# A graph network on one core: edge terms are placed in the ring and the gathers add node rows to them

## The chip, the cores and the metric

The kernel runs on one core of a Trainium2 chip. Its time is the device time of one execution, in microseconds (us); lower is better. The time before is the median of three runs. Engines are named as in the profile: PE is the matrix engine (PEld its weight loads), DVE the vector engine, ACT the scalar engine, POOL the engine that issues the gathers, SP the engine that only issues transfers.

## What is computed

A layer norm with a ReLU, an encoder, three message passing layers over 212,500 edges of 12,500 nodes, and an output product over all four hidden states, with a residual:

```python
h = jnp.maximum(_layernorm(x), 0.0)
h_list = [h @ enc_w + enc_b]
for l in range(3):
    e = edge_attr @ edge_w[l] + edge_b[l]            # 212500 x 128 from 212500 x 16
    msg = relu(h_list[l][src] + e)
    agg = segment_sum(msg, dst, num_segments=12500)  # edges are sorted by dst
    z = (1.0 + eps[l]) * h_list[l] + agg
    z = relu(z @ mlp_w1[l] + mlp_b1[l]) @ mlp_w2[l] + mlp_b2[l]
    h_list.append(relu(z))
out = x + concatenate(h_list) @ out_w + out_b
```

Everything is float32.

## The kernel before

**Tiling.** The edges are cut into tiles of 128, and four tiles make a group (`TG`), so a layer has `NG` = 416 groups, the last with one tile, and three layers have 1248 groups and 4983 tiles. Node sums live transposed in SBUF (`agg_t`, 128 features by 12,500 nodes). The edges of a group are sorted by destination and fall in a window of 64 nodes (`WIN`) that begins at a base read from a table.

**A group's work.** (1) SP loads the edge attributes, eight groups at a time (`attr`, two halves). (2) POOL gathers the source rows from `h_table` in HBM, one indirect transfer per tile (L372), into a slot of `rows`, a ring of `RING` = 16 slots. (3) PE multiplies the attributes by the edge weights into a PSUM bank (`edge_terms`, L620; three banks `e_ps`). (4) DVE adds the bank to the gathered rows in place (`add_terms`, L879) and makes a one-hot matrix of the destinations (`one_hot`, L865). (5) ACT applies the ReLU in place (L543). (6) PE multiplies the rows by the one-hot matrix, four tiles summed in one bank (`window_sums`, L624; two banks `agg_ps`). (7) DVE adds the 64 columns to `agg_t` (`add_window`, L875).

**Order.** Each engine's order is written by hand; a body of 16 groups is looped on all engines but POOL, whose 416 groups are written out. In a body of before PE does the edge terms of group k+2 and then the sums of group k. DVE does the one-hot matrix of group k, then `add_window` of group k-2, then `add_terms` of group k, so these three wait in that order for one another. POOL waits, before the first tile of a group, for the sums of the group 16 back (semaphore `agg_done`), since they free the slot.

**Node work.** When all edges of 512 nodes are summed, a table says so and the three products of those nodes are put into the same loops (a unit of node work: PE `node_z`, `node_h`, `node_out`; ACT `relu_z`, `relu_h`; DVE `node_take`). Two banks, `zh_ps` and `zt_ps`, serve it. The new node rows go to the other `h_table` by a transfer that ACT issues. The next layer's gathers wait for all of them (semaphore `stored`).

**Start.** After the layer norm the first eight groups of layer 0 are gathered while the encoder's products (`h0_turned`, `o0`) run; the next eight wait for tables that DVE makes (`find_units`, L813); the seventeenth waits for the first group's sums.

## Time and profile before

| | us |
|---|---|
| median of 3 runs | 7389.25 (7386.51 to 7396.62) |
| the profiled execution's own time | 7395.73 |
| its span, first to last instruction | 7393.9 |

| engine | busy us | share |
|---|---|---|
| PE | 4774.5 | 65% |
| POOL | 4751.3 | 64% |
| PEld | 3131.3 | 42% |
| DVE | 1663.8 | 23% |
| ACT | 999.7 | 14% |

The mean granted clock of PE is 0.558 of full speed: most stretches are at the lower of its two levels. Transfers keep the 16 DMA engines busy for about a fifth of the span. No engine is busy for the whole span, so the shares alone do not name the bound; the waits and the timeline do. An engine's idle time stands in square brackets behind the instruction that it waited to begin, with what ended it; "remote" is a release that the profile cannot pin on an instruction, and "issue" is time in which it sees nothing that was waited for. The ends of PE's instructions are modelled, not measured.

### The profile page before, as it was taken

To read this page: it belongs to the slowest core of one execution; us is meant where nothing else is said; L and a number is where in the kernel's file an instruction comes from. 1 tells how busy PE (TensorE), PEld (TensorE's weight loads), DVE (VectorE), ACT (ScalarE), POOL (GpSimd) and SP (SyncE) were. 2 spreads that over 40 slices of the span, in tenths; PEclk is the share of its full clock that TensorE was granted. 3 is DMA by queue.
4 is the path that set the end of the run, shared out by engine and by line. 5 is a ranking of instruction groups with operands and counts; after the bars stand their busy time and mean duration, and the time that the engine had idled before them with its cause. 6 is when DMAs were issued, how large, how long until landed. Compare 5 with 4: busy or idle time off the path is not lost.

```text
span 7393.9 us, 56283 instructions
## 1 busy us (share of the span) xinstructions
PE 4774.5 (65%) x14396; PEld 3131.3 (42%) x14397; DVE 1663.8 (23%) x4168; ACT 999.7 (14%) x1597; POOL 4751.3 (64%) x5075
## 2 busy tenths in 40 slices
PE   5666666666666646666666666673666666666667
PEld 4444444444444424444444444442444444444444
DVE  4222222222222212222222222221222222222222
ACT  4111111111111101111111111110111111111111
POOL 5666666666666466666666666646666666666664
PEclk7555555555555555555555555555555555555555
DMA  3122212222222112222222222211111111111112
GB/s 116 53 54 54 55 53 54 54 55 54 54 54 54 44 49 54 55 55 54 54 55 55 53 54 56 55 43 51 51 51 52 51 52 51 52 51 51 52 52 72
DMA packets 191126, 404.82 MB, mean 55 GB/s; under 512 B 85159, under 2 KB 87927, under 8 KB 190439
## 3 DMA queue, kind: packets, MB, share of 16 engines
q0 software_dynamic: 159456, 326.88, 17.0%
q1 hardware_dynamic: 21759, 56.75, 2.6%
q10 hardware_dynamic: 9840, 20.48, 0.8%
q14 instruction: 55, 0.45, 0.0%
q8 instruction: 16, 0.26, 0.0%
HBM read 378.08 MB, written 25.69 MB: 55 GB/s over the span
## 4 chain that ended last, share of the span: by engine, by line
another core or an unknown queue 44%; PE 27%; issue 18%; DVE 6%; DVEq 3%; ACT 3%; POOL 0%; DMA 0%; ACTq 0%
PE bank L624 14%; PE bank L620 9%; DVE rows L879 3%; ACT rows L543 2%; DVE onehot L865 2%; PE bank L651 1%; PE bank L664 1%; PE bank L643 1%; DVEq L939 1%; DVE agg_t L875 1%; PE bank L645 1%; DVEq L247 1%; DVEq L875 0%; PE bank L661 0%
## 5 line engine op out<-in xcount | busy, mean ns | idle before, releaser
L372 POOL DMA_INDIRECT rows<-h_table,idx x4983 | 4714.0, 946 | 2575.5 <-issue 1417.7
L624 PEld LDWEIGHTS bank<-onehot,rows 128*128 128x128 f32 x9966 | 2178.6, 310 | 3367.3 <-ACT rows L543 1966.2
L624 PE MATMUL bank<-onehot,rows 128*128 128x64 f32 x9966 | 2158.1, 394 | 2162.8 <-ACT rows L543 1599.7
L620 PE MATMUL bank<-edgew,attr 65*128 65x512 f32 x2496 | 2279.0, 1026 | 9.6 <-DMA w2s<-w 9.6
L543 ACT ACTIVATE rows<-rows 128x512 f32<-128x512 f32 x1248 | 783.1, 628 | 5381.1 <-DVE rows L879 4213.0
L875 DVE TENSOR_TENSOR agg_t<-bank,agg_t 128x64 f32 x1248 | 278.1, 223 | 4790.4 <-remote 3542.9
L879 DVE TENSOR_TENSOR rows<-bank,rows 128x512 f32<-128x512 f32 x1248 | 857.6, 687 | 83.2 <-DMA rows<-h_table,idx 35.2
L620 PEld LDWEIGHTS bank<-edgew,attr 65*128 65x128 f32 x2496 | 677.7, 316 | 280.6 <-issue 280.6
L865 DVE TENSOR_TENSOR onehot<-bank,dst_rel 128x256 f32<-128x256 f32 x1248 | 518.3, 415 | 205.4 <-issue 205.4
L651 PE MATMUL bank<-hid,w2s 128*128 128x512 f32 x300 | 195.3, 769 | 192.5 <-ACT hid L506 124.8
L664 PE MATMUL bank<-outw,h_t 128*128 128x128 f32 x588 | 151.7, 423 | 62.0 <-ACT h_t L515 58.5
L506 ACT ACTIVATE hid<-bank,b1s 128x512 f32<-128x512 f32 (+1 forms) x150 | 101.0, 678 | 539.1 <-remote 297.3
L664 PEld LDWEIGHTS bank<-outw,h_t 128*128 128x128 f32 x588 | 142.5, 326 | 64.2 <-ACT h_t L515 60.4
L651 PEld LDWEIGHTS bank<-hid,w2s 128*128 128x128 f32 x300 | 59.8, 233 | 256.5 <-ACT hid L506 155.7
L643 PE MATMUL bank<-agg_t,w1s 128*128 (+1 forms) x150 | 149.1, 1097 | 1.7 <-DVE agg_t L875 1.7
L645 PE MATMUL bank<-agg_t,w1s 128*128 (+1 forms) x150 | 124.5, 928 | 0.0
L661 PE MATMUL bank<-ident,h_t 128*128 128x128 f32 x196 | 45.6, 372 | 107.2 <-ACT h_t L515 100.7
L916 DVE COPY h_n<-bank 128x512 f32<-128x512 f32 (+1 forms) x50 | 34.1, 681 | 356.3 <-remote 242.8
L515 ACT ACTIVATE h_t<-bank,b2s 128x512 f32<-128x512 f32 (+1 forms) x75 | 50.9, 678 | 369.1 <-remote 232.3
L922 DVE TENSOR_TENSOR out_acc<-bank,out_acc 128x512 f32 (+1 forms) x75 | 50.6, 674 | 199.3 <-remote 101.8
L645 PEld LDWEIGHTS bank<-agg_t,w1s 128*128 128x128 f32 x150 | 50.3, 335 | 74.9 <-issue 74.4
L661 PEld LDWEIGHTS bank<-ident,h_t 128*128 128x128 f32 x196 | 33.7, 224 | 112.1 <-ACT h_t L515 104.8
(83 smaller groups left out, 478.6 us busy)
## 6 DMA issues: line engine op xcount, KB each, us to landing
rows<-h_table,idx POOLq DMA_INDIRECT x4983
attr<-ea_t SPq DMA_DIRECT2D x156, 256.0 KB
h_table<-h_n ACTq DMA_DIRECT2D x48, 256.0 KB
h_table<-rows SPq DMA_DIRECT2D x24, 256.0 KB, 2.1
out<-out_acc SPq DMA_DIRECT2D x24, 256.0 KB
out_acc<-x_t ACTq DMA_DIRECT2D x4, 1280.0 KB, 11.5
rows<-dst_g SPq DMA_DIRECT2D x1, 832.0 KB
rows<-dst_t SPq DMA_DIRECT2D x1, 832.0 KB
```

The costliest lines, as they stand in the source:

```text
L372: return g.indirect_dma_start(dst, None, h_table[l % 2], bass.IndirectOffsetOnAxis(ap=index, axis=0))
L506: nc.scalar.activation(hid[:, c, 0:cols], ps[:, 0:cols], ACT.Relu, bias=b1s[:, l * HC + c:l * HC + c + 1])\
L543: nc.scalar.activation(part, part, ACT.Relu).then_inc(relued, 1)
L620: return nc.tensor.matmul(dst[0:EP, 0:tiles * D], cols, edgew[:, l, 0:tiles * D], start=True, stop=True)
L624: last = nc.tensor.matmul(dst[:, 0:WIN], rows[0:EP, slot, j, :], onehot[0:EP, hot_slot, j, :], start=(j == 0), stop=(j == tiles - 1))
L643: nc.tensor.matmul(zh_ps[:, 0:cols], w1s[:, 0:D], moving, start=True, stop=True).then_inc(z_done, 1)
L645: nc.tensor.matmul(zt_ps[:, 0:cols], w1s[:, D:2 * D], moving, start=True, stop=True).then_inc(z_done, 1)
L651: last = nc.tensor.matmul(zh_ps[:, 0:cols], w2s[:, c, :], hid[:, c, 0:cols], start=(c == 0), stop=(c == HC - 1))
L664: last = nc.tensor.matmul(zh_ps[:, j * D:(j + 1) * D], cols[:, j, :], outw[:, l + 1, :], start=True, stop=True)
L865: return v.tensor_tensor(onehot[0:EP, slot, 0:tiles, :], numbers[0:EP, :].unsqueeze(1).broadcast_to([EP, tiles, WIN]), dst_rel[0:EP, bass. ...
L875: return v.tensor_tensor(cols, ps[:, 0:WIN], cols, ALU.add)
L879: return v.tensor_tensor(part, ps[0:EP, 0:tiles * D].rearrange("p (t d) -> p t d", d=D), part, ALU.add)
```

## The change

Four parts.

1. **Edge terms go into the ring first, and the gather adds.** PE now does the edge terms of group k+8 (`AHEAD`) before the sums of group k, in four banks instead of three. DVE copies the bank into the slot of `rows` (`place`, semaphore `placed`) and no longer adds. The gather of a group waits for `placed` of that group and carries the operation add: it adds the node rows to what is in the slot. ACT waits for the gather itself (`gathered`), and DVE no longer waits for a gather.
2. **Four groups' sums share a bank.** `window_sums` writes 64 columns for each of four groups side by side, and `agg_done` rises once for the four. DVE adds the four windows in a row and makes the four next one-hot matrices (now eight slots, semaphore `hot_made`). The table of column numbers is kept in both banks of sums.
3. **SP issues the stores of node rows**, and in the last layer the stores of the output, inside its loop. ACT issues none. The attributes of the first groups of a layer are loaded, placed and made one-hot at the end of the layer before.
4. **Banks and the start.** The encoder's stage uses other banks: two for `o0` instead of four, and the output bias is read from SBUF. The first eight groups are placed inside that stage, one after each of its first eight steps, so that the first gather waits for the first placing.

The core of the diff:

```diff
-NE_PS = 3
+NE_PS = 4
+AHEAD = 8
+BATCH = 4
-NHOT = 4
+NHOT = 2 * BATCH
...
-            def gather(l, dst, index):
-                return g.indirect_dma_start(dst, None, h_table[l % 2], bass.IndirectOffsetOnAxis(ap=index, axis=0))
+            def gather(l, dst, index, op=ALU.bypass):
+                return g.indirect_dma_start(dst, None, h_table[l % 2], bass.IndirectOffsetOnAxis(ap=index, axis=0),
+                                            compute_op=op)
...
-                    if l == 0 and group == HB:
-                        g.wait_ge(s_ready, 1)
-                    if l or group >= RING:
-                        g.wait_ge(agg_done, l * NG + group + 1 + S0 - RING)
+                    g.wait_ge(placed, l * NG + group + 1 + S0)
...
-                        gather(l, rows[0:EP, slot, t % TG, :], idx[0:EP, t:t + 1]).then_inc(gathered[slot], 16)
+                        gather(l, rows[0:EP, slot, t % TG, :], idx[0:EP, t:t + 1], ALU.add).then_inc(gathered[slot], 16)
...
-                        act.wait_ge(summed, b * RING + (l * NG + k + 1 + S0))
+                        act.wait_ge(gathered[k], (b + (l * uses_of_slot(k) + 1)) * (16 * TG))
...
+            def e_terms(l, b, k):
...
+                pe.wait_ge(placed, b * RING + (l * NG + k + 1 - NE_PS + S0))
+                edge_terms(e_ps[k % NE_PS], attr[half][:, kk * EP:(kk + 1) * EP], l, real_tiles(b, k))\
+                    .then_inc(e_done, 1)
...
+                def sums(b, k):
+                    batch, i = k // BATCH, k % BATCH
+                    if i == 0:
+                        pe.wait_ge(hot_made, b * (RING // BATCH) + (l * NQ + batch + 1 + S0))
+                    pe.wait_ge(relued, b * RING + (l * NG + k + 1))
+                    last = window_sums(agg_ps[batch % NA_PS][:, i * WIN:(i + 1) * WIN], k, k % NHOT, real_tiles(b, k))
+                    if i == BATCH - 1:
+                        last.then_inc(agg_done, 1)
...
+            def place(l, b, k):
+                tiles = real_tiles(b, k)
+                dve.wait_ge(e_done, b * RING + (l * NG + k + 1 + S0))
+                v.tensor_copy(rows[0:EP, k, 0:tiles, :],
+                              e_ps[k % NE_PS][0:EP, 0:tiles * D].rearrange("p (t d) -> p t d", d=D)).then_inc(placed, 1)
...
                 with nc.Fori(0, NFULL, engines=(mybir.EngineType.DVE,), hint_back_edge=True) as b:
+                    load_bases(b, 0)
+                    first_places(l, b, 3)
+                    accumulate(b, 0)
+                    one_hots(b, 2)
+                    last_places(l, b, 3)
+                    take_unit(b * 2)
+                    first_places(l, b + 1, 0)
+                    accumulate(b, 1)
+                    one_hots(b, 3)
+                    last_places(l, b + 1, 0)
...
```

How the orders differ is shown best by the instructions themselves. On DVE, groups 2 and 3 of a body before: the one-hot matrix (L865), the window of the group two back (L875), the addition to the gathered rows (L879), with what each waits for.

```order
L865 TENSOR_TENSOR onehot<-bank,dst_rel 128x256
L931 REGISTER_ALU [waits agg_done]
L875 ISA [waits added]
L875 TENSOR_TENSOR agg_t<-bank,agg_t 128x64
L944 REGISTER_ALU
L879 TENSOR_TENSOR rows<-bank,rows 128x512 [waits gathered2,e_done]
L865 ISA
L865 TENSOR_TENSOR onehot<-bank,dst_rel 128x256
L875 ISA [waits added,agg_done]
L875 TENSOR_TENSOR agg_t<-bank,agg_t 128x64
L944 REGISTER_ALU
L879 TENSOR_TENSOR rows<-bank,rows 128x512 [waits gathered3,e_done]
```

On DVE now, the beginning of a body: two placings of groups 12 and 13 (L875 is `place` there), one wait for the sums of groups 0 to 3, the first two of their four windows (L906).

```order
L875 COPY rows<-bank 128x512 [waits e_done]
L874 REGISTER_ALU
L875 COPY rows<-bank 128x512 [waits e_done]
L971 ISA
L973 ISA [waits agg_done]
L906 ISA [waits added]
L906 TENSOR_TENSOR agg_t<-bank,agg_t 128x64
L973 ISA
L906 ISA [waits added]
L906 TENSOR_TENSOR agg_t<-bank,agg_t 128x64
```

A wait for a gather and an instruction of its own for the addition have gone; the wait for sums stands once for four groups, with the placings on both sides of it.

On PE, two groups of a body before: the edge terms wait for nothing of their own, the sums for the ReLU.

```order
L620 MATMUL bank<-edgew,attr 128x512
L686 REGISTER_ALU
L624 MATMUL bank<-onehot,rows 128x64 [waits relued]
L624 MATMUL bank<-onehot,rows 128x64 x3
L620 MATMUL bank<-edgew,attr 128x512
L686 REGISTER_ALU
L624 MATMUL bank<-onehot,rows 128x64 [waits relued]
L624 MATMUL bank<-onehot,rows 128x64 x3
```

On PE now, groups 0 and 1 of a body, with the edge terms of groups 8 and 9.

```order
L621 MATMUL bank<-edgew,attr 128x512 [waits placed]
L700 ISA
L701 REGISTER_ALU [waits hot_made]
L646 MATMUL bank<-onehot,rows 128x64 [waits relued]
L646 MATMUL bank<-onehot,rows 128x64 x3
L627 REGISTER_ALU
L621 MATMUL bank<-edgew,attr 128x512 [waits placed]
L701 REGISTER_ALU
L646 MATMUL bank<-onehot,rows 128x64 [waits relued]
L646 MATMUL bank<-onehot,rows 128x64 x3
```

The matmuls are the same in kind and number; each edge term now waits until the group four back has been placed, and sits eight groups ahead of the sums instead of two.

## Rows read from the trace of the kernel before

**Rows 1.** The page, parts 1 and 4: busy time, and the chain that ended last.
```profile
PE 4774.5 (65%) x14396; PEld 3131.3 (42%) x14397; DVE 1663.8 (23%) x4168; ACT 999.7 (14%) x1597; POOL 4751.3 (64%) x5075
another core or an unknown queue 44%; PE 27%; issue 18%; DVE 6%; DVEq 3%; ACT 3%; POOL 0%; DMA 0%; ACTq 0%
```

**Rows 2.** Waits of POOL (total, times, longest us); then L372: duration ns min/median/max.
```profile
POOL rows L372 <- remote: 903.0, 305, 10.6
POOL rows L372 <- DMA h_table<-h_n: 119.7, 2, 62.7
POOL rows L372 <- PE bank L624: 107.5, 59, 30.7
...
L372 POOL DMA_INDIRECT rows<-h_table,idx x4983: 942/947/1138, 58.0 to 7339.6; - x200
```

**Rows 3.** Timeline of POOL (start, us, instruction, idle before), layer 0, two ring waits.
```profile
2016.98 0.95 POOL L372 DMA_INDIRECT rows<-h_table,idx  x1 [0.30 <-issue]
2021.21 0.95 POOL L372 DMA_INDIRECT rows<-h_table,idx  x1 [3.28 <-remote]
...
2044.98 0.94 POOL L372 DMA_INDIRECT rows<-h_table,idx  x1 [0.30 <-issue]
2049.82 0.94 POOL L372 DMA_INDIRECT rows<-h_table,idx  x1 [3.90 <-remote]
```

**Rows 4.** Timeline of PE in the same stretch.
```profile
2008.20 1.81 PE L624 MATMUL bank<-onehot,rows 128*128 128x64 f32 x8
...
2013.21 2.02 PE L620 MATMUL bank<-edgew,attr 65*128 65x512 f32 x2
2022.75 1.97 PE L624 MATMUL bank<-onehot,rows 128*128 128x64 f32 x8 [7.52 <-ACT rows L543]
```

**Rows 5.** Timeline of DVE in the same stretch.
```profile
2008.22 0.41 DVE L865 TENSOR_TENSOR onehot<-bank,dst_rel 128x256 f32<-128x256 f32 x1
2021.17 0.23 DVE L875 TENSOR_TENSOR agg_t<-bank,agg_t 128x64 f32 x1 [12.53 <-remote]
```

**Rows 6.** DVE and POOL after layer 1's start; PE in two stretches (us, busy, clock).
```profile
2571.47 0.23 DVE L875 TENSOR_TENSOR agg_t<-bank,agg_t 128x64 f32 x1 [13.47 <-remote]
...
2599.47 0.23 DVE L875 TENSOR_TENSOR agg_t<-bank,agg_t 128x64 f32 x1 [26.80 <-issue]
...
2627.70 0.22 DVE L875 TENSOR_TENSOR agg_t<-bank,agg_t 128x64 f32 x1 [27.03 <-remote]
...
2650.78 0.95 POOL L372 DMA_INDIRECT rows<-h_table,idx  x1 [10.43 <-remote]
...
2021.00:2035.00 14.00, 12.25 (x39) 0.50 0.19 47
2571.00:2599.00 28.00, 3.78 (x10) 0.50 0.21 54
```

**Rows 7.** Timeline of POOL and DVE: the start, the gap between layers, the last gather.
```profile
118.63 0.94 POOL L372 DMA_INDIRECT rows<-h_table,idx  x1 [20.72 <-DVEq L813]
...
189.05 0.95 POOL L372 DMA_INDIRECT rows<-h_table,idx  x1 [30.71 <-PE bank L624]
...
184.92 0.68 DVE L879 TENSOR_TENSOR rows<-bank,rows 128x512 f32<-128x512 f32 x1
...
2535.57 0.95 POOL L372 DMA_INDIRECT rows<-h_table,idx  x1 [62.70 <-DMA h_table<-h_n]
...
7339.65 0.95 POOL L372 DMA_INDIRECT rows<-h_table,idx  x1 [0.30 <-issue]
```

**Rows 8.** Groups by line and form (count, busy us, mean ns, idle before); then the gathers' queue.
```profile
L879 DVE TENSOR_TENSOR rows<-bank,rows 128x512 f32<-128x512 f32 x1245 | 856.7, 688 | 83.2 <-DMA rows<-h_table,idx 35.2 <-remote 27.7 <-issue 14.8
L916 DVE COPY h_n<-bank 128x512 f32<-128x512 f32 x48 | 33.2, 692 | 346.0 <-remote 242.8 <-PE bank L661 51.9 <-issue 51.3
...
q0 software_dynamic: 159456, 326.88, 17.0%
```

More of the change, by code:

```diff
@@ L903, in _ @@
             dve.wait_ge(o0_added, NI)
-            own(v.tensor_copy(iota_ps, iota[:, :]))
             dve.wait_ge(seeded0, NI)
+            for ps in iota_ps:
+                own(v.tensor_copy(ps, iota[:, :]))
             n_far = load_extra(dve)
@@ new lines, in load_bases, with take_unit @@
+                def load_bases(b, half):
+                    dve.load(bases[half * HB:(half + 1) * HB], base_row[0:1, bass.ds(b * RING + half * HB, HB)])
+                def take_unit(hb):
+                    unit = load_unit(dve, hb)
+                    with dve.If(unit > 0):
+                        node_take(unit_before(unit))
+                if l == 0:
+                    one_hots(0, 0)
+                first_places(l, 0, 2)
+                last_places(l, 0, 2)
+                one_hots(0, 1)
```

264 lines of the change are left out of this document (148 added, 116 removed).

## The prediction

> **What bounds the kernel now.** I read the busy shares and the chain first. No engine is above 65%, and the largest share of the chain, 44%, is "another core or an unknown queue" [rows 1], so the chain does not name the bound. Next come the waits and the timeline of POOL, since each of the 4983 gathers is an instruction of its own. A gather holds POOL for 947 ns in the median, hardly ever more [rows 2], and where nothing is waited for 0.30 us pass between two [rows 3]. That is 1.252 us per gather with the 0.305 us that the gap measures over a long row, 5.01 us per group of four. This is the floor of the gathers: 4983 x 1.252 = 6237 us of 7394.
>
> What is added to it are waits of POOL. Twice it waits for the stored rows of a new layer, 119.7 us together. The others are waits for a free slot of the ring: 903.0 us in 305 waits and 107.5 us in 59 [rows 2], of which one, 30.7 us, belongs to the start [rows 7]. Each of the 363 left has an ordinary gap of 0.30 in it, so they cost 903.0 + 107.5 - 30.7 - 109 = 871 us. The first 16 groups lie before 189.05 us, so this is spread over 1232 groups: 0.71 us per group. A loop of 16 slots should not run dry with an engine that is 5.01 us per group and others that are faster, so I ask what is late.
>
> At 2008.20 PE starts the sums of a group; by the profile they end at 2010.01, and PE's work goes on to 2015.2 and then stops for 7.52 us, waiting for a ReLU [rows 4]. DVE waits meanwhile, 12.53 us, to add the window of exactly those sums, and does it at 2021.17 [rows 5]. POOL had gathers to issue until 2016.98, then waited 3.28 us and went on at 2021.21 [rows 3]. So the completion of PE's work reached the others some 11 us after its modelled end, about 3 us after POOL had fallen idle. The next round is the same: POOL idle from 2045.92, going on at 2049.82. After the start of layer 1, where the ring is empty and POOL issues from 2535.57 [rows 7] for more than 100 us without a stop, until a wait that ends at 2650.78 [rows 6], DVE gets PE's sums 28 us apart (2571.47, 2599.47, 2627.70), and PE issues 3.78 us of work in 28 us, against 12.25 in 14 us elsewhere, both at 0.50 of full clock [rows 6]. I do not know the mechanism. What the rows show is a **rule of thumb**: under a long unbroken run of gathers PE's completions come late, and most come in once POOL pauses. Every round trip from PE over DVE and ACT back to PE is stretched by that, and in this kernel DVE's order makes one every two groups: the addition of group k stands behind the window of group k-2.
>
> So time = gathers + ring waits + start + two layer gaps + tail. The tail is from the last gather's end at 7340.6 to 7393.9, 53.3 us [rows 7]. Check: 189.05 + (4983 - 64) x 1.252 + 871 + 119.7 + 53.3 = 7391.6, for a span of 7393.9. I carry the 2.3 us left over along.
>
> **The change, part by part.**
>
> *The addition moves into the gather.* DVE loses 1248 additions of 688 ns (857 us) and gains 1248 copies out of PSUM. A copy of the same shape out of a bank costs 692 ns [rows 8], so DVE's busy time stays, 23%, beside other work: zero. ACT's work is unchanged. What POOL and the transfer pay for the add no row shows. Transfer: the gathers' queue takes 17.0% of the DMA engines [rows 8], so even with three times the work per row it would take about half, and a later landing is covered by the eight groups (40 us) between a placing and its use: zero. POOL: below, a gather that adds can't be cheaper than one that does not, 947 ns. From above, the longest gather in the trace is 1138 ns, 191 ns more [rows 2]. I take 947, since the length is the same to a few ns in 4983 cases and did not depend on where data goes; but each 0.01 us more is 4951 x 0.01 = 50 us on the path, with no cover at all. This is the weakest point of the forecast.
>
> *The ring.* POOL waited for sums 16 groups back, now it waits for the placing of the same group. Since PE does the edge terms of group k+8 just ahead of the sums of group k, POOL can be about eight groups ahead of the sums instead of 16. PE's own run-ahead without an answer from others grows from two groups to four: an edge term needs only the placing four back, and the sums of four groups give one signal. Queued behind DVE's new wait for four sums are two placings, which POOL waits for, so a late completion reaches POOL through one instruction more. From rows 3 a round was 5 groups and a wait of 3.90 us. I estimate a round of 8 groups: the three that complete in time at the head of a run, four of run-ahead, and one more that trickles in. The wait in it: 3.90, plus one placing with its signal (0.69 + 0.2), less the ordinary gap of 0.30, so 4.5 us, 0.56 per group. Bounds: no waits at all, 0; as now, 0.71.
>
> *Start.* Before, 16 groups had been gathered when the loop began, at 189.05. Now POOL may not begin at 58 us but once the first placing is done, in the encoder's stage, and holds eight placings until that stage ends. The ninth comes where now the first addition stands, at 184.92 [rows 7], with 0.69 for the copy: 186 us. So eight groups remain that were hidden, 8 x 5.01 = 40 us lost. The tables that DVE makes at the seventh step of that stage are ready at 118.63 [rows 7], and placing starts with the first step, so I put the first gather at 100 us; the first eight groups (40 us) then end before 186 and cost nothing. The waits of POOL for tables (20.72) and for the first sums (30.71) go, but they are inside those 186 us.
>
> *Gaps and tail.* The stored rows are still waited for at a layer's start, 119.7 us; that SP issues the stores in place of ACT moves an issue, and the rows are late through the node work itself. SP's waits for node rows now stand ahead of its next load of attributes, which is asked for eight groups (40 us) before its use: covered. Tail 53.3. Both the pre-loading of attributes and the two banks fewer for `o0` are hidden in the same stage or gap: zero.
>
> Sum: 186 + (4983 - 32) x 1.252 (6199) + 1240 x 0.56 (694) + 119.7 + 53.3 + 2.3 = 7254 span. The profiled execution took 1.8 us more than its span and 6.5 more than the median: 7254 + 1.8 - 6.5 = **7250 us**, 1.9% faster.
>
> **The rivals.**
>
> *The gather that adds costs POOL more (slower).* Place: L372, 4951 times on the path. It decides from (7254 against 7394) 140 / 4951 = 0.028 us per gather: 3% more than 947 ns turns the gain into a loss. At the row's upper end, +0.191, it is 7250 + 946 = 8196. In the middle, +0.10, 7745. For it: an add has to name a second source for every row, and POOL does that naming. Against it: nothing in the trace. Should the whole 947 ns double, 4951 x 0.947 = 4689 more, 11,940; the row says only that this is a fixed length, not what it consists of.
> *The waits vanish.* If four groups' run-ahead is enough for PE never to be late for POOL, the ring term is 0: 7250 - 694 = 6556. For it: one signal per four groups. Against it: in the long run of rows 6 sums that waited for no one came 28 us apart, so it isn't the round trips alone. Half way it would be 6900.
>
> *The waits stay as they are.* If POOL must fall idle every five groups for PE's sake, whatever the lead, the ring term is 1240 x 0.71 = 880 and the time 7250 + 186 = 7436, 0.6% slower, by the 40 us lost at the start.
>
> *The halved lead bites.* After a long run POOL finds fewer placings in store, and each wait runs through PE, DVE's order and back. At a wait like the longest ring wait, 10.6 us [rows 2], every 8 groups, it is 1240 / 8 x 10.3 = 1597 in place of 694: 8150. There are 1240 / 8 = 155 rounds; it decides from (694 + 140) / 155 = 5.4 us a round, or 5.7 with the ordinary gap.
>
> **How the numbers follow.** Forecast case (price within 0.02 us, fewer waits) 0.42; price higher 0.32, of it 0.06 beyond 8200; waits gone or nearly 0.09; waits as now 0.10; lead bites 0.07. Faster: nearly all of 0.42 and 0.09, less what of the forecast lies near zero, 0.48. Within 0.2%, about what a measurement can tell from no change: 0.06, from the edge of the forecast and of "as now". Slower 0.46. The likeliest single case is on the faster side though the two sides weigh nearly the same. Its own range is 7050 to 7385. The range for all reaches down half way to no waits, 6800, and up to the longest gather of the row, 8200.
>
> **What would show it.** In the profile after: the mean of a gather on L400, 947 ns or more, and the gap between two; this alone decides the sign. POOL's waits in total and how many there are: about 155 of 4.8 us (694 and the gaps) if I am right. DVE's copies at 0.69 us with waits for PE, and its wait for four sums; ACT's waits now end with gathers. First gather after 100 us instead of at 58, the ninth group at 186. Layer gaps near 60 us each. The forecast is wrong if a gather takes 3% more, if PE's completions are as late with a lead of eight, or if an adding transfer lands so late (over 30 us) that the lead is gone.

## The result and the profile after

| | before | after |
|---|---|---|
| median, same chip | 7392.93 us (7386.51 to 7403.84) | 9355.59 us (9350.57 to 9356.86) |
| ratio | 1 | 1.2655, 95% interval 1.2639 to 1.2671 |
| span of the profiled execution | 7393.9 us | 9348.7 us |

The changed kernel is 26.5% slower. The prediction was 7250 us, with a range from 6800 to 8200. It was wrong in sign and size. Below, a time without a ratio is that of one execution, and ratios leave out disturbed executions (one, of the filler kernel that was measured again, took 15,293 us beside five of 7368 to 7379 us).

The page of after, parts 1, 3 and 4, against [rows 1] and the queue's row in [rows 8]:

```profile
PE 5148.1 (55%) x14396; PEld 3051.7 (33%) x14397; DVE 1716.0 (18%) x4168; ACT 990.5 (11%) x1597; POOL 7737.5 (83%) x5076
...
q0 software_dynamic: 717552, 326.88, 29.1%
...
POOL 81%; issue 16%; PE 1%; DVE 1%; DMA 0%; ACT 0%; SPq 0%; POOLq 0%; DVEq 0%; ACTq 0%
```

POOL is busy for 7737.5 us instead of 4751.3. The chain of work that ended last, whose largest share (44%) named no engine before, is now POOL (81%) and the gap behind each of its instructions (16%). The gathers' queue moves the same 326.88 MB in 717,552 packets, 144 per gather where it had been 32.

The line of the gathers in after (duration ns min/median/max, first and last start), then POOL's waits, against [rows 2]:

```profile
L400 POOL DMA_INDIRECT rows<-h_table,idx x4983: 1535/1544/2777, 79.0 to 9332.5; - x200
```
```profile
POOL rows L400 <- issue: 1515.6, 4976, 0.3
POOL rows L400 <- DMA h_table<-h_n: 37.9, 2, 19.6
POOL rows L400 <- DVE rows L875: 29.4, 5, 28.1
```

A gather that adds takes 1544 ns in the median instead of 947. The ring waits (1010 us in 364 waits before) are gone: five waits for a placing are left, and one of them, 28.1 us, stands before the very first gather. The timeline of POOL in after shows the new beat, 1.85 us, without a break where [rows 3] had a pause every five groups:

```profile
3000.57 1.54 POOL L400 DMA_INDIRECT rows<-h_table,idx  x1 [0.30 <-issue]
3002.42 1.54 POOL L400 DMA_INDIRECT rows<-h_table,idx  x1 [0.30 <-issue]
3004.27 1.54 POOL L400 DMA_INDIRECT rows<-h_table,idx  x1 [0.30 <-issue]
```

The whole span follows from it: first gather at 79.0, 4982 steps of (9332.5 - 79.0 - 37.9) / 4982 = 1.850 us, two layer gaps of 37.9 together, and 16.2 from the last gather's start to the end.

The others wait for POOL. The largest waits of ACT and DVE in after, against the waits on PE in [rows 5] and [rows 6]:

```profile
ACT rows L556 <- DMA rows<-h_table,idx: 8266.6, 1241, 12.1
```
```profile
DVE rows L875 <- PE bank L621: 7342.7, 1195, 11.4
DVE agg_t L906 <- PE bank L646: 33.0, 2, 26.3
```

The windows (L906) wait for PE's sums twice in the whole kernel; in before DVE waited for them up to 27 us at a time [rows 6]. PE's lateness has gone with the ring waits.

### The profile page after: what moved, and what is told of

It reads as the page before. It is cut to its first block, busy times and chain, and to the rows that moved or that the text cites. A ratio compares the mean times of both kernels' runs of the same rounds, so it can differ in the third digit from the quotient of the medians.

```text
span 9348.7 us, 55192 instructions
## 1 busy us (share of the span) xinstructions
PE 5148.1 (55%) x14396; PEld 3051.7 (33%) x14397; DVE 1716.0 (18%) x4168; ACT 990.5 (11%) x1597; POOL 7737.5 (83%) x5076
## 3 DMA queue, kind: packets, MB, share of 16 engines
q0 software_dynamic: 717552, 326.88, 29.1%
## 4 chain that ended last, share of the span: by engine, by line
POOL 81%; issue 16%; PE 1%; DVE 1%; DMA 0%; ACT 0%; SPq 0%; POOLq 0%; DVEq 0%; ACTq 0%
POOL rows L400 81%; PE bank L621 0%; PE bank L646 0%; PE bank L608 0%; PE bank L600 0%; DVE onehot L762 0%; DMA rows<-h_table,idx 0%; DMA rows<-dst_g 0%; PE bank L686 0%; PE bank L673 0%; PE bank L593 0%; DMA out_acc<-x_t 0%; PE bank L665 0%; DMA h_table<-h_n 0%; PE bank L683 0%
## 5 line engine op out<-in xcount | busy, mean ns | idle before, releaser
L400 POOL DMA_INDIRECT rows<-h_table,idx x4983 | 7700.4, 1545 | 1582.8 <-issue 1515.6
L646 PE MATMUL bank<-onehot,rows 128*128 128x64 f32 x9966 | 2336.3, 412 | 4130.1 <-ACT rows L556 4129.6
L646 PEld LDWEIGHTS bank<-onehot,rows 128*128 128x128 f32 x9966 | 2112.3, 313 | 5918.8 <-ACT rows L556 5841.6
L621 PE MATMUL bank<-edgew,attr 65*128 65x512 f32 x2496 | 2303.9, 1023 | 13.8 <-issue 13.5
L875 DVE COPY rows<-bank 128x512 f32<-128x512 f32 x1248 | 861.0, 690 | 7356.6 <-PE bank L621 7342.7
L621 PEld LDWEIGHTS bank<-edgew,attr 65*128 65x128 f32 x2496 | 654.5, 313 | 146.1 <-issue 145.2
L896 DVE TENSOR_TENSOR onehot<-bank,dst_rel 128x256 f32<-128x256 f32 x1248 | 441.2, 416 | 1.0 <-DVE bank L937 1.0
L906 DVE TENSOR_TENSOR agg_t<-bank,agg_t 128x64 f32 x1248 | 277.4, 222 | 162.1 <-PE bank L646 33.0
L673 PE MATMUL bank<-hid,w2s 128*128 128x512 f32 x300 | 261.7, 1026 | 0.0
L673 PEld LDWEIGHTS bank<-hid,w2s 128*128 128x128 f32 x300 | 90.9, 334 | 77.0 <-issue 74.4
L667 PEld LDWEIGHTS bank<-agg_t,w1s 128*128 128x128 f32 x150 | 50.5, 337 | 74.9 <-issue 74.4
L665 PEld LDWEIGHTS bank<-agg_t,w1s 128*128 128x128 f32 x150 | 40.8, 332 | 11.9 <-issue 11.9
```

Of the source, the lines that this page charges most:

```text
L400: return g.indirect_dma_start(dst, None, h_table[l % 2], bass.IndirectOffsetOnAxis(ap=index, axis=0), compute_op=op)
L621: return nc.tensor.matmul(dst[0:EP, 0:tiles * D], cols, edgew[:, l, 0:tiles * D], start=True, stop=True)
L646: last = nc.tensor.matmul(dst, rows[0:EP, slot, j, :], onehot[0:EP, hot_slot, j, :], start=(j == 0), stop=(j == tiles - 1))
L665: nc.tensor.matmul(zh_ps[:, 0:cols], w1s[:, 0:D], moving, start=True, stop=True).then_inc(z_done, 1)
L667: nc.tensor.matmul(zt_ps[:, 0:cols], w1s[:, D:2 * D], moving, start=True, stop=True).then_inc(z_done, 1)
L673: last = nc.tensor.matmul(zh_ps[:, 0:cols], w2s[:, c, :], hid[:, c, 0:cols], start=(c == 0), stop=(c == HC - 1))
```

## The experiments

The kernel before took between 7393 and 7452 us, with most of the difference between one chip and another, so each kernel is compared with the kernel before on the same chip in the same session. The traces of the kernel before (7393.9 us of span) and of the variants come in part from different chips; small differences between them, of the order of 1%, are not read as effects.

### Is it the gather, the order, or both?

The changed kernel with a plain gather (the edge terms in the ring are overwritten, that is, left out of the sum):

```diff
-  gather(l, rows[0:EP, slot, t % TG, :], idx[0:EP, t:t + 1], ALU.add).then_inc(gathered[slot], 16)
+  gather(l, rows[0:EP, slot, t % TG, :], idx[0:EP, t:t + 1]).then_inc(gathered[slot], 16)
```

> The changed kernel with one thing undone: the gather carries no add, it overwrites the placed edge terms (so the messages lack their edge terms; the order, the waits and the count of instructions are those of the changed kernel). Theory A: the whole loss is the price of the adding gather, 1545 ns against 947, and the new order by itself has ended the ring waits. Then gathers are 947 ns again and the span is 79 (first gather) + 4983 x 1.252 (6239) + 38 (layer gaps) + about 30 (waits for placings at the start) + 15 (tail) = about 6400 us. Theory B: the ring waits went only because the gathers became slower or came with other transfers; with gathers every 1.25 us PE's completions are late again and POOL waits for placings, by my prediction some 700 us in all: 7000 to 7300 us.

Measured: 7456.63 us, before 7452.4, ratio 1.001 (1.0 to 1.0019). That is theory B in kind, but above its range: the waits came back, and more of them than expected. The line of its gathers and POOL's waits:

```profile
L400 POOL DMA_INDIRECT rows<-h_table,idx x4983: 938/944/2199, 78.6 to 7429.4; - x200
```
```profile
POOL rows L400 <- issue: 1452.3, 4711, 2.5
POOL rows L400 <- DVE rows L875: 1168.0, 270, 36.6
POOL rows L400 <- DMA h_table<-h_n: 54.8, 2, 28.5
```

Of the 1168 us two waits belong to the start: 28.0 us before the first gather, and 36.6 us before the ninth group's, which the timeline of POOL shows:

```profile
158.10 0.94 POOL L400 DMA_INDIRECT rows<-h_table,idx  x1 [36.57 <-DVE rows L875]
```

Without these and the ordinary gap of 0.30 in each of the other 268, about 1020 us of ring waits are left, none longer than 7.5 us.

The other half: the kernel before, in its own order, with a gather that adds from the 17th group on (the values are not those wanted, since DVE adds the edge terms as well).

```diff
-  gather(l, rows[0:EP, slot, t % TG, :], idx[0:EP, t:t + 1]).then_inc(gathered[slot], 16)
+  gather(l, rows[0:EP, slot, t % TG, :], idx[0:EP, t:t + 1],
+         ALU.add if l or group >= RING else ALU.bypass).then_inc(gathered[slot], 16)
```

> The kernel before with one thing changed: from the seventeenth group on the gather adds to what the slot still holds (left-over messages, so the values differ), DVE still adds the edge terms. Theory A: the price belongs to the gather and to nothing in the new order, so a gather takes 1.54 us here too; if the ring waits belonged to the old order (0.71 us a group, 871 us in all) they stay, and the time is 7390 + 4919 x 0.598 = 10,300 us. Theory B: the slower gathers themselves end the ring waits; then it is 9400 to 9500 us with hardly a wait of POOL for PE.

Measured: 9355.97 us, the time of the changed kernel to 0.4 us (this is one execution, beside 7452.4 us for the kernel before). Theory B holds in kind; the time is just below its range. POOL's waits there, and its gathers:

```profile
POOL rows L372 <- issue: 1517.8, 4975, 0.3
POOL rows L372 <- PE bank L626: 31.0, 4, 30.1
POOL rows L372 <- DMA h_table<-h_n: 28.0, 2, 15.8
```
```profile
L372 POOL DMA_INDIRECT rows<-h_table,idx x4983: 940/1549/1595, 57.7 to 9339.7; - x200
```

The two together: the operation in the gather is the whole slowdown, and the new order, the shared banks and SP's stores taken together are worth nothing measurable without it. The ring waits go in either order when the gather adds, and stay in either order when it does not. So the order, for which my forecast had found a gain of 186 us in the waits, does not decide over them.

### What does a gather's length consist of?

The changed kernel with gathers of 64 rows in place of 128, once adding and once plain (half of the node rows are left out; in the plain one the edge terms under the other half too):

```diff
-  gather(l, rows[0:EP, slot, t % TG, :], idx[0:EP, t:t + 1], ALU.add).then_inc(gathered[slot], 16)
+  gather(l, rows[0:64, slot, t % TG, :], idx[0:64, t:t + 1], ALU.add).then_inc(gathered[slot], 16)
```

> The changed kernel with gathers of 64 rows instead of 128 (half of the node rows are left out), with the add. If the 1545 ns are a fixed part and a part per row, this gives the split; a plain gather of 64 rows is to follow. If the add is priced per row (a second source for each row) the gather takes between 773 and 1250 ns; if the add costs a fixed amount more, it takes about 598 ns more than a plain one of 64 rows. The time follows as about 4983 x (gather + 0.30) + 140.

> The changed kernel with plain gathers of 64 rows (no add, half of the node rows left out). With 1412 ns for an adding gather of 64 rows and 1545 for one of 128, the add has 2.1 ns a row and 1279 ns fixed. Price theory 1 (the add costs a fixed amount, whatever the rows): a plain gather of 64 rows takes 1412 - 598 = 814 ns. Price theory 2 (the add costs per row): the plain one is then near 947 - 64 x 2.1 or less steep, 880 to 947 ns. Its gathers come faster than any so far if the fixed part is small, so ring waits should be at least those of new_plain_gather (1168 us) if the pace of the gathers is what makes PE late, and fall if it is the rows moved.

Measured: 8692.32 us adding (before 7452.4), 7431.34 plain (before 7395.4). The gathers of the adding kernel, then of the plain one:

```profile
L400 POOL DMA_INDIRECT rows<-h_table,idx x4983: 1402/1411/2122, 79.1 to 8674.4; - x200
```
```profile
L400 POOL DMA_INDIRECT rows<-h_table,idx x4983: 898/904/1624, 78.3 to 7405.5; - x200
```

From 64 to 128 rows a plain gather grows by 40 ns (904 to 944), 0.6 ns per row; an adding one by 133 ns (1411 to 1544), 2.1 ns per row. If a straight line through the two lengths holds down to no rows, that leaves 864 and 1278 ns. By this estimate some 414 of the 600 ns that adding costs here are a fixed part and some 186 go with the rows, so neither of the two expected prices (all fixed, all per row) was right. The packets of a gather are 144 at 128 rows and 80 (398,640 / 4983) at 64, which fits 16 and one per row, while the plain one has 32 at either length.

The plain kernel with half the rows brought a surprise: POOL's gathers were shorter and the transfers half as large (163.6 MB instead of 326.88), and the time stayed: 0.5% above its kernel before, where whole gathers gave 0.1%. So the ring waits (1295.1 us, counted like the 1168) do not come from bytes.

### Why are there ring waits at all?

In both orders a gather of 1.85 us beat ended them. Does the slower beat do it, or the add? The kernel before with a memset on POOL behind each gather, which POOL waits for:

```diff
+        filler = sb("filler", [P, 128])
...
         gather(l, rows[0:EP, slot, t % TG, :], idx[0:EP, t:t + 1]).then_inc(gathered[slot], 16)
+        g.memset(filler[:, :], 0.0).then_inc(s_fill, 1)
+        filled += 1
+        g.wait_ge(s_fill, filled)
```

> The kernel before with a small memset of POOL (128 columns) after every gather, waited for, so that plain gathers come more slowly. It asks whether the pace of the gathers or their being one after the other makes PE's completions late. If pace or unbroken gathers are the cause, the ring waits (903 + 107 us) fall to near nothing though order and transfers are those of before, and the time is the number of gathers times their new distance plus about 300 us. If the cause is in the order of the loops, the waits per round remain (0.7 us a group).

Measured: 7367.81 us (before 7452.4). The beat is 0.95 + 0.22 + 0.27 = 1.44 us, and the waits for a slot are gone:

```profile
POOL rows L374 <- issue: 979.8, 3310, 1.9
POOL rows L374 <- POOL filler L407: 450.1, 1660, 0.3
POOL rows L374 <- DMA h_table<-h_n: 26.7, 2, 14.7
...
POOL rows L374 <- PE bank L630: 9.0, 5, 7.9
```

The same edit, measured again:

> The kernel before with a memset of 128 columns, waited for, after each gather, as in the earlier run of the same edit, which gave 7367.8 in one execution beside 7452 for the kernel before in the same hour. This is to tell whether the slower pace is faster than the kernel before. Theory P: POOL at 1.44 us per gather is at PE's pace, so the time is the kernel before's within 0.5%, with almost no waits. Theory R: fewer late completions, 0.5 to 1% faster than before.

Measured: 7375.45 us, before 7449.0, ratio 0.9892 (0.9863 to 0.992); the two medians alone give 0.990. POOL does 1088 us more work and the kernel is about 1% faster. It is the only complete version found that beats both kernels, and a small gain.

The gain does not come from the gathers. From the first to the last, without the layer gaps, they go at 1.459 us each, no faster than in the trace of before (1.437, see the table below; that trace is from another chip, but the 56 us that the kernel before took longer on this one are at most 0.011 us per gather). What shrank are the two layer gaps, from 119.7 us to 24.6, and the time from the last gather's end to the end of the kernel, from 53.3 us to 13.1. The likely reason is that PE is no longer behind when a layer ends. POOL's two waits for the stored rows of a layer:

```profile
POOL rows L374 <- DMA h_table<-h_n: 24.6, 2, 12.7
```

Is it the unbroken run of gathers, or their beat? The same memset once per group, behind the fourth gather (beat 1.30 us in the mean); then a memset of one column behind each gather (0.945 + 0.113 + 0.27 = 1.33 us); then 64 columns (0.951 + 0.166 + 0.27 = 1.39 us).

```diff
+                    g.memset(filler[:, 0:128], 0.0).then_inc(s_fill, 1)
+                    filled += 1
+                    g.wait_ge(s_fill, filled)
...
+                        g.memset(filler[:, 0:1], 0.0).then_inc(s_fill, 1)
...
+        filler = sb("filler", [P, 64])
...
+                        g.memset(filler[:, :], 0.0).then_inc(s_fill, 1)
```

> The kernel before with one memset of POOL (0.22 us, waited for) after the four gathers of a group. Theory P (pace): PE is late when gathers come 1.25 us apart and not at 1.44; at a mean of 1.30 it stays late and the ring waits fall only a little: 7200 to 7450 us. Theory U (unbroken runs): any other POOL instruction between gathers lets PE's completions through, so one in four is enough: no ring waits, 4983 x 1.252 + 1248 x 0.19 + 300 = 6780 us, which would beat both kernels.

> The kernel before with a memset of one column after each gather. The memset itself may take about 0.1 us, a gather then comes every 1.35 us. Theory P: if the limit lies between 1.25 and 1.35 us the ring waits go and the time is 4983 x 1.35 + 190 = 6900 us; if it lies above, some waits remain and the time is between 6900 and 7400. Theory U: no waits, 6900 us.

> The kernel before with a memset of 64 columns, waited for, after each gather: about 1.385 us per gather, between the runs with 1 column (1.33 us, 7479) and with 128 (1.44 us, 7368 and 7375). Without waits it would be 4983 x 1.385 + 190 = 7090. Theory Rate with its limit just under 1.44: the waits fill up to the same pace, 7370 to 7480. If the limit is below 1.385: 7090 to 7150, and that is a version 4% faster than before.

Measured: 7476.74 us, ratio 1.0108 (1.0088 to 1.0128); 7478.98 us, ratio 1.0113 (1.0093 to 1.0134); 7500.21 us, ratio 1.0078 (1.006 to 1.0096). All three are slightly slower than the kernel before, and each lies 20 to 80 us above the range that the pace theory had given. In all three the waits for a slot are there, shrinking as the beat grows: the rows with "remote" of POOL's waits, in the kernel with one column and in that with 64:

```profile
POOL rows L374 <- remote: 518.7, 204, 3.9
```
```profile
POOL rows L374 <- remote: 268.4, 145, 3.2
```

A break in the run does not help by itself. What POOL spends on fillers comes off its waits, and the sum nearly stays.

In the new order with plain gathers the fillers, once per group and once per gather (edge terms left out as above), gave:

> The changed kernel's order with plain gathers (edge terms are overwritten and so left out) and one memset after each group. It asks what the new order is worth once PE's completions are in time. Theory U: about 6700 us, since its layer gaps are 38 us and its tail is short, against 6780 for the old order. Theory P: 7200 to 7450, POOL still waits about 1000 us for placings.

> The changed kernel with plain gathers, so that they overwrite the edge terms, which are thus left out, and with the memset of 128 columns, waited for, after each gather (1.44 us per gather). Both theories: POOL's waits for a placing fall from 1168 us to under 150. Time 79 + 4983 x 1.44 (7176) + 38 + 16 + the waits = 7310 to 7460. If it is under 7330, the order of the changed kernel is worth about 1% once the gathers are paced.

Measured: 7467.88 us (waits for a placing 894.9 us in 259; before 7395.4) and 7423.39 us (39.9 in 9; before 7449.0). The new order has nothing to add once the gathers are spaced: with the same filler, on the same chip, the old order took 7375.

### Is it PE's own pace?

If PE needed longer than its modelled ends say, it would be the second bound, close above POOL. Half of its sums left out (two of a group's four tiles are summed), all gathers kept:

```diff
             def window_sums(dst, slot, hot_slot, tiles=TG):
+                tiles = min(tiles, 2)
                 for j in range(tiles):
```

> The kernel before with all its gathers, but the sums use only the first two of the four tiles of a group: half of the sums is left out. PE's modelled work falls by half of 2158 us of the sums and half of their weight loads. Theory P (PE's true pace is the second bound, just above the gathers'): PE comes in time, POOL's waits for a slot vanish, and the time is the floor of the gathers with start, layer gaps and tail: 6200 + 189 + 120 + 53 = 6560 (6500 to 6750). Theory R (the gathers make completions late whatever PE does): POOL's waits stay 700 to 1000 us and the time 7250 to 7400.

And half of the gathers left out, all of PE's work kept (the count is made up on the semaphore):

```diff
+                    if tiles == TG and (l or group >= RING):
+                        tiles = TG // 2
                     if tiles < TG:
                         g.inc_swdge_sem([gathered[slot]], [16 * (TG - tiles)], mode="add")
```

> The kernel before, but from the 17th group on only the first two tiles of a full group are gathered; the other two keep the rows that an earlier group left there, so half of the node rows are left out. PE, DVE and ACT do all their work. POOL now has 2 x 1.25 = 2.5 us of work per group. If PE's completions come late because of the gathers (Theory R: POOL and the transfers disturb the others), PE finishes in time and the time falls far, to the PE work of 4775 us busy and some waits, 5000 to 6200 us. If the pace of 1.44 us per gather (5.8 us per group) that all plain runs come back to is the real pace of the round trip PE, DVE, ACT (Theory P: PE takes longer than its modelled ends say), the time stays near 7300 (7100 to 7400) and POOL waits for a slot most of the time, about 1232 x 3.2 = 4000 us.

Measured: 7369.82 us with half the sums (before 7449.0), and 4593.52 us with half the gathers. Busy times of the first, its waits for a slot, and busy times of the second:

```profile
PE 3885.9 (53%) x9416; PEld 2161.1 (29%) x9417; DVE 1667.8 (23%) x4168; ACT 996.8 (14%) x1597; POOL 4751.7 (64%) x5075
```
```profile
POOL rows L372 <- remote: 921.9, 299, 9.3
```
```profile
PE 4254.6 (93%) x14396; PEld 2870.2 (63%) x14397; DVE 1670.8 (36%) x4168; ACT 998.9 (22%) x1597; POOL 2420.1 (53%) x2617
```

PE lost 889 us of work, the kernel 1.1% (one execution), and the waits stayed: 921.9 us where before has 903.0. Without half of the gathers PE was busy for 93% of the time and did all its work in 4592 us, which is below the 5000 to 6200 us that I had expected. Its mean granted clock was 0.64 there instead of 0.558, and its busy time 4255 us instead of 4775; even at the busy time of before, 93% would be an estimated 5134 us. So PE, DVE and ACT can go at 3.7 us per group (about 4.1 at the clock of before); what keeps them at 5.8 comes with the gathers.

### A pace per gather, or per group?

Three gathers of four (the fourth tile keeps an earlier group's rows), first with the semaphore filled up by an instruction of POOL's in each group, alone, with one memset of 992 columns per group, and with the 128 columns behind each gather:

```diff
+                    three = tiles == TG and (l or group >= RING)
+                    if three:
+                        tiles = 3
                     if tiles < TG:
                         g.inc_swdge_sem([gathered[slot]], [16 * (TG - tiles)], mode="add")
```

> The kernel before, but from the 17th group on the fourth tile of a full group is not gathered, so a quarter of the node rows is left out. POOL's work is 3 x 1.25 = 3.76 us per group; PE, DVE and ACT do all theirs, which with half the gathers took them 4592 us for the whole kernel. Theory Rate (PE's completions come late as soon as gathers follow each other faster than 1.44 us on average): 3 x 1.44 = 4.32 us per group, 1232 x 4.32 + 360 for start, layer gaps and tail = 5680 (5500 to 5800), with waits of POOL of about 700 us. Theory Group (what has to be kept is a time per group, 5.8 us, whatever is gathered): 7100 to 7400. If the waits vanish altogether: 1232 x 3.76 + 360 = 4990.

> As old_three_gathers, and a memset of 992 columns, waited for, in place of the fourth gather, so that POOL is occupied for about as long as before (a gather 0.95 us; the memset by the rows of the 1 and the 128 columns 113 + 992 x 0.84 = 950 ns), but issues a quarter fewer gathers: 5.0 us per group, 1.67 us per gather. Theory Rate: no ring waits, 1232 x 5.0 + 360 = 6520 (6400 to 6700). Theory Busy (it is POOL's being occupied without a stop that makes the others late, whatever with): the waits stay at about 900 us, 7250 to 7450.

> As old_three_gathers (the fourth tile of a full group not gathered, 6072.5 us), and the memset of 128 columns, waited for, after each of the three gathers, so POOL has more to do: 3 x 1.44 = 4.32 us per group in place of 3.76. Theory Spacing (gathers that follow each other closely make PE's completions late, and a distance of 1.44 us is enough to end it, whatever the rest costs): no ring waits, 1232 x 4.32 + 360 = 5680 (5600 to 5780), 6% faster with more work for POOL. Theory Rate of a group (a group with three gathers can't go faster than the 4.63 us that it took, for a reason that lies outside POOL): 6000 to 6150, with waits of POOL of about 400 us.

Measured: 6072.52, 7762.15 and 7365.44 us. None lies in a range that a theory gave, and the timeline of POOL in the third tells why the last two can't be used:

```profile
3007.89 0.95 POOL L374 DMA_INDIRECT rows<-h_table,idx  x1 [1.64 <-issue]
3008.84 0.22 POOL L409 MEMSET filler<- 128x128 f32 x1
3009.33 0.95 POOL L374 DMA_INDIRECT rows<-h_table,idx  x1 [0.27 <-POOL filler L409]
3010.29 0.22 POOL L409 MEMSET filler<- 128x128 f32 x1
3010.78 0.95 POOL L374 DMA_INDIRECT rows<-h_table,idx  x1 [0.27 <-issue]
3011.73 0.22 POOL L409 MEMSET filler<- 128x128 f32 x1
3013.62 0.95 POOL L374 DMA_INDIRECT rows<-h_table,idx  x1 [1.67 <-issue]
```

Before the first gather of each group 1.6 us pass instead of 0.27: the instruction that fills up the semaphore, which stands between the filler's wait and that gather. It was part of my edit, not of the question. So I made the edit without it (DVE waits for 48 per use instead of 64), alone and with the 128 columns behind each gather:

```diff
-                    if tiles < TG:
-                        g.inc_swdge_sem([gathered[slot]], [16 * (TG - tiles)], mode="add")
+                    if tiles < 3:
+                        g.inc_swdge_sem([gathered[slot]], [16 * (3 - tiles)], mode="add")
...
-                        dve.wait_ge(gathered[k], (b + (l * uses_of_slot(k) + 1)) * (16 * TG))
+                        dve.wait_ge(gathered[k], (b + (l * uses_of_slot(k) + 1)) * 48 + 16)
```

> As old_three_gathers (the fourth tile of a full group not gathered), but DVE waits for a count of 48 per use in place of 64, so that POOL need not add to the semaphore by an instruction of its own in each group. It is the base for old_three_paced_clean. Its gathers were 0.30 us apart with that instruction too, so the time should stay at 6072 (6000 to 6120) with POOL's waits for a slot near 1200 us. If the instruction was what made the others late there, the time falls to the floor, 1232 x 3.76 + 360 = 4990.

> old_three_clean with the memset of 128 columns, waited for, after each gather; in old_three_paced the instruction that adds to the semaphore stood on POOL's path for 1.3 to 1.7 us per group and hid the answer (7365 us). Now 3 x 1.44 = 4.32 us per group. Theory Spacing (a distance of 1.44 us ends the late completions whatever the rest costs): no ring waits, 1232 x 4.32 + 360 = 5680 (5600 to 5780), 6% faster than old_three_clean though POOL has more to do. Theory Other bound (a group with three gathers can't go faster than 4.63 us for a reason outside POOL): 6000 to 6150, with waits of POOL of about 400 us.

Measured: 5760.9 and 5777.31 us (before 7452.02). The first expectation missed: the instruction had cost 6070.7 - 5759.1 = 311.6 us of span. It did not cost this evenly. Before most groups (880 of 1228) the gap is 0.30 us with the instruction, as it is without it (791). Where POOL waited for a slot, the trace has the instruction only after the wait, and the gather another 1.4 to 2.1 us after it (median 1.7): in the following row of the first kernel the instruction stands at 3008.98, the gather starts at 3010.37. The second was in its range, but as the base had moved there too, the spacing gained nothing, and some waits for a slot stayed. That row, then POOL's waits for a slot in the two clean kernels, alone and with the filler:

```profile
3010.37 0.95 POOL L372 DMA_INDIRECT rows<-h_table,idx  x1 [3.88 <-issue]
```

```profile
POOL rows L372 <- remote: 611.1, 275, 9.8
POOL rows L372 <- PE bank L627: 379.5, 358, 30.7
```
```profile
POOL rows L374 <- remote: 96.7, 72, 1.9
POOL rows L374 <- PE bank L632: 59.9, 42, 8.0
```

POOL did 820 us of memsets more and waited 834 us less. A quarter fewer gathers made the kernel 23% shorter: the pace is one per gather, not per group.

### All of them side by side

The beat that POOL could keep (its instructions and the ordinary gap), and the one that it kept, from the first gather's start to the last, without the two layer gaps, over the number of steps:

| kernel | could, us | kept, us |
|---|---|---|
| new order, plain, 64 rows | 1.21 | 1.459 |
| before | 1.25 | 1.437 |
| half the sums | 1.25 | 1.438 |
| new order, plain | 1.25 | 1.464 |
| three gathers of four, clean | 1.25 | 1.473 |
| filler per group | 1.30 | 1.457 |
| new order, plain, filler per group | 1.30 | 1.465 |
| filler of 1 column | 1.33 | 1.458 |
| filler of 64 columns | 1.39 | 1.461 |
| filler of 128 columns | 1.44 | 1.459 |
| new order, plain, filler of 128 columns | 1.44 | 1.464 |
| three of four, 128 columns | 1.44 | 1.480 |
| new order, adding, 64 rows | 1.71 | 1.718 |
| after | 1.85 | 1.850 |
| old order, adding | 1.85 | 1.858 |

For before, (7339.6 - 58.0 - 119.7) / 4982 = 1.437. Up to 1.44 us the kept beat lies at 1.44 to 1.48, whatever POOL could do; beyond, it is POOL's own. This holds over two orders, 64 and 128 rows, whole and half sums, three and four gathers in a group. Left out of the table are the kernel with half of the gathers, where PE at 93% is the bound, and the three that carry the added instruction in each group, which kept 1.586, 1.943 and 2.049 us. In this kernel **the average over the whole run is at best 1.44 to 1.48 us per gather**, and what is issued faster for a while is paid back in waits.

**Not the transfers.** One suspect is that the transfers work off a gather more slowly than POOL issues it. The trace of before speaks against it. Stretches of before (us, busy of PE, PEld, DVE, ACT and POOL, PE's clock, DMA share, GB/s): the long run after the start of layer 1, then the run and the wait of POOL of [rows 3]:

```profile
2535.00:2651.00 116.00, 31.93 (x76) 17.29 (x76) 8.74 (x22) 4.41 (x7) 79.69 (x85) 0.50 0.20 52
2005.00:2017.00 12.00, 10.24 (x24) 5.47 (x23) 2.38 (x5) 1.26 (x2) 8.95 (x11) 0.50 0.20 51
2017.00:2019.20 2.20, 0.00 (x0) 0.00 (x0) 0.00 (x0) 0.00 (x0) 0.93 (x1) 0.50 0.24 60
2019.30:2021.20 1.90, 0.00 (x0) 0.00 (x0) 0.03 (x1) 0.00 (x0) 0.00 (x0) 0.50 0.00 0
```

From 2019.3 on nothing moves any more, and yet POOL waits until 2021.21. The packets of the gathers' queue in the same trace, 32 to a gather, say it for the whole kernel: the first one starts 1.65 us after its gather and the last one ends 1.24 us after POOL's part, in the median in before, in the new order with plain gathers and in the filler kernel alike. In the long run after 2535, 84 gathers and their packets both follow at 1.251 us, with the same 1.65 us at its begin and at its end. So the transfers keep up at 1.25 us; of the 336 gaps of POOL above 0.45 us from 200 us on, 93% ended when the last packet of the last gather was already through, in the median 1.87 us after it.

**What stays open.** Late are the completions of PE that DVE and POOL wait for. Whether PE's work itself ends late or only its signals arrive late can't be told, since PE's ends are modelled; nor do the runs say which part holds them back, or why that comes to 1.44 us per gather. It is not the bytes, the transfers, the sums, the ring's order or a missing break.

## Why the prediction was wrong

**The step that failed is the price of the gather.** I wrote "I take 947, since the length is the same to a few ns in 4983 cases and did not depend on where data goes". It is 1544. The constancy of a number over cases in which the operation never changed says nothing about another operation. The text had named it "the weakest point of the forecast" and had worked out that 0.028 us would turn the sign; it was 0.60. The upper bound, 191 ns from the longest plain gather, was no bound for an add: it was the scatter of another thing. Of the two outer prices in that rival, +0.191 and a doubling, the measured +0.597 lies between, at 63% of 947.

**The ring waits.** Forecast: 155 rounds of 4.8 us, from a lead counted in groups. Measured: none. Nor were they the 694 of the forecast or the 880 of "as now" in the new order with a plain gather, but about 1020. The model of round trips was wrong. In every plain kernel the waits filled up the difference between the beat that POOL could keep and 1.44 to 1.48 us, so the 6237 us were a floor that neither order came near: in plain form the new order gave 7452.7 of span against 7254. The rival "the waits stay as they are" (7436, 0.6% slower) comes nearest to what happened without the add (0.1% slower).

**The sum in the right terms.** 1.44 us per gather was already being paid. The 0.60 us of the add ended the waits (871 us), the layer gaps fell from 119.7 to 37.9 and the tail from 53.3 to 14.7 after the last gather's end, and the rest is the loss. The 65th gather started at 200.3 us instead of 189.1; from it on 4919 x 0.597 = 2937. With the 11 us of the start, less 871, 82 and 39, that makes 1956; the span grew by 1954.8.

**Right.** DVE's work stayed (1716 us against 1664; a placing takes 690 ns, estimated 692), ACT's too (990.5 against 999.7); a later landing and the moves of SP's issues cost nothing on POOL's path, where no wait names them. The rival of the halved lead was not put to a test in after, since a gather of 1.85 us beat hardly caught up with the placings. In the plain kernel it can be read: past the start no wait for a placing is longer than 7.5 us, where that rival had 10.6 every eight groups, but there are more of them than the 155 rounds that it had, and the waits together (about 1020 us) lie between the forecast's 694 and its 1597.

**Start and gaps.** The first gather began at 79.0, not 100, and the ninth group did not wait for 186. Its placing came much earlier, at 140.03, and with the slower beat eight groups last 62 us, so its gather started at 141.09 without a gap:

```profile
140.03 0.69 DVE L875 COPY rows<-bank 128x512 f32<-128x512 f32 x1 [0.49 <-PE bank L621]
```
```profile
141.09 1.54 POOL L400 DMA_INDIRECT rows<-h_table,idx  x1 [0.30 <-DVE rows L875]
```

With plain gathers the loss at the start is there (36.6 us until 158.10, against 40 estimated, though its end had been put at 186). The layer gaps are 19 us each, not 60. The forecast had laid them to the node work itself, but in the filler kernel, whose order is that of before, they are 12 us each. So most of a gap was not the node work but, as far as the waits tell, PE's lateness when a layer ends.

## What to carry to other kernels

An operation that rides along in a transfer is paid where the transfer is issued. If that engine is the bound, measure one such instruction first: here an addition that took 857 us of a vector engine at 23% made POOL's gathers 2986 us longer (4714.0 to 7700.4 us), and the copy that replaced it on the vector engine took as long as the addition had. And before taking waits as recoverable, slow the engine that waits on purpose: if a filler makes the waits shrink and the time stay, the pace has its limit elsewhere, and a faster order may not find it.

## What the runs showed of the hardware

- An indirect gather of 512-byte rows held POOL for 904 ns at 64 rows and 944 to 947 at 128. With the operation add it was 1411 and 1544 ns, with 80 and 144 packets instead of 32.
- Plain gathers averaged 1.44 to 1.48 us each over a whole kernel, though POOL could issue one every 1.21 to 1.39 us. Their transfers kept up with 1.251 us over a run of 84 gathers; PE's sums reached DVE 28 us apart in that run.
- Slowing POOL to 1.44 us made the kernel about 1% faster (0.9892, 0.9863 to 0.992), by shorter layer gaps and a shorter tail.
- A memset on POOL of 1, 64, 128 and 992 columns took 113, 166, 218 and 942 ns.
- The instruction on POOL that adds to a gather's semaphore cost nothing that shows within a run of gathers (the gap stays 0.30 us), and 1.4 to 2.1 us (median 1.7) where it stands behind a wait of POOL.
